# Spare matmuls on TensorE in the entry of a two-layer AdaLN kernel (17 of them, ahead of three waits)

## The reference, cut to what matters

```python
mod = (silu(c) @ wmod).reshape(8, 6, 1, 128)       # sa, ca, ga, sb, cb, gb
ga, gb = sign(.) * maximum(abs(.), 0.25)           # the two gates are clipped
h = layernorm(x) * (1 + ca) + sa
x = x + ga * attention(h)     # layer 0: 16 heads of 8, W + 2 * A.T B.T (LoRA) for q, k, v, o
h = layernorm(x) * (1 + cb) + sb
x = x + gb * moe(h)           # layer 0: 8 experts, top 2, and one shared; layer 1: SSM, conv + MoE
```

## Time and profile before

| | us |
|---|---|
| median of 3 runs | 1002.78 (998.81 to 1006.16) |
| the profiled execution | 1009.28 |
| its span, first to last instruction | 1007.5 |
| its mean granted TensorE clock | 0.909 |
| PE, DVE, ACT, POOL busy | 840.4, 738.3, 632.3, 496.3 |

### The profile page before, as it was taken

The page is one execution under the profiler, slowest core; times in us unless marked ns, Lnnn a source line. Parts: engine busy times, 40 slices in busy tenths (PEclk is TensorE's granted clock), DMA queues, the critical chain, the costliest instruction groups (busy, mean ns, idle before and its releaser), DMA issues.

```text
span 1007.5 us, 14225 instructions
## 1 busy us (share of the span) xinstructions
PE 840.4 (83%) x4630; PEld 461.7 (46%) x4630; DVE 738.3 (73%) x1561; ACT 632.3 (63%) x1113; POOL 496.3 (49%) x794
## 2 busy tenths in 40 slices
PE   5689999999988988887796999889946559977986
PEld 4312222222212222221475877777733247766774
DVE  6687878788888778862485888858749577966771
ACT  2157777877766777676484777566715736545562
POOL 3715282727265666355552167656657046653211
PEclk9669999999999999898798999999967878978997
DMA  7735454545536264102115266556360000000000
GB/s 238 153 107 186 91 182 97 166 112 152 125 120 160 107 172 124 68 24 109 52 36 177 97 221 247 195 190 217 115 237 10 24 1 1 0 1 11 22 21 32
DMA packets 45477, 110.78 MB, mean 110 GB/s; under 512 B 7886, under 2 KB 20814, under 8 KB 40086
## 3 DMA queue, kind: packets, MB, share of 16 engines
q1 hardware_dynamic: 39260, 97.93, 32.5%
q0 software_dynamic: 4992, 10.36, 3.0%
q10 hardware_dynamic: 1152, 1.58, 0.5%
HBM read 57.65 MB, written 51.03 MB: 108 GB/s over the span
## 4 chain that ended last, share of the span: by engine, by line
PE 49%; DVE 19%; issue 10%; POOL 10%; ACT 8%; DMA 4%; SPq 0%; another core or an unknown queue 0%; POOLq 0%; DVEq 0%; ACTq 0%
PE PS L1083 10%; DVE mx L891 9%; PE PS L1072 6%; PE PS L1053 4%; PE PS L320 4%; PE PS L322 3%; PE PS L321 3%; POOL yd L1298 3%; DMA HT<-xs 2%; ACT E L798 2%; PE PS L1035 2%; PE PS L1020 1%; ACT ov L804 1%; PE PS L2425 1%; PE PS L2428 1%
## 5 line engine op out<-in xcount | busy, mean ns | idle before, releaser
L891 DVE TENSOR_REDUCE mx<-PS 128x2 f32<-128x1024 f32 x256 | 305.5, 1221 | 76.4 <-PE PS L1053 70.6
L798 ACT ACTIVATE E<-PS 128x512 f32<-128x512 f32 x512 | 277.0, 599 | 85.8 <-PE PS L1072 81.7
L1072 PE MATMUL PS<-Q,K 51*128 51x512 bf16 x512 | 166.0, 396 | 10.6 <-ACT E L798 6.9
L1053 PE MATMUL PS<-K,Q 48*128 48x512 bf16 x512 | 140.6, 409 | 27.1 <-DVE mx L891 26.7
L1083 PE MATMUL PS<-E,V 128*9 128x512 f32 x1024 | 140.1, 620 | 19.5 <-ACT ov L804 18.8
L1298 POOL DMA_INDIRECT yd<-yt,goes x92 | 94.6, 1028 | 49.2 <-DVE yt L1474 25.6
L1072 PEld LDWEIGHTS PS<-Q,K 51*128 51x128 bf16 x512 | 37.0, 95 | 162.1 <-ACT E L798 97.2
L1462 DVE TENSOR_TENSOR Gl<-Gf,Gh 128x512 fp32r<-128x512 f32 x117 | 82.2, 719 | 31.6 <-ACT Gh L1333 22.1
L513 POOL DMA_INDIRECT xs<-HT,pos x64 | 63.8, 996 | 79.5 <-ACT E L798 45.2
L1327 ACT ACTIVATE Gf<-PS,WR 128x512 f32<-128x512 f32 x92 | 63.1, 689 | 48.7 <-PE PS L322 39.3
L2336 DVE SCALAR_TENSOR_TENSOR cb<-ye,gt,cb 128x128 f32<-128x128 f32 x224 | 65.5, 366 | 0.0
(11 more groups left out here) (420 smaller groups left out, 1895.1 us busy)
## 6 DMA issues: line engine op xcount, KB each, us to landing
WR<-wsd SPq DMA_DIRECT2D x23, 1028.0 KB
xs<-zero SPq DMA_DIRECT2D x8, 2112.0 KB, 7.4
wsd<-wsp SPq DMA_DIRECT2D x8, 1024.0 KB, 4.1
HT<-xs SPq DMA_DIRECT2D x23, 264.0 KB
dqk<-SPL SPq DMA_DIRECT2D x30, 192.0 KB, 2.8
Q<-dqk SPq DMA_DIRECT2D x14, 384.0 KB
K<-dqk SPq DMA_DIRECT2D x14, 384.0 KB
stage<-in_w SPq DMA_DIRECT2D x9, 516.0 KB
```

The costliest lines, as they stand in the source:

```text
L798: e.activation(E[:, m % 4, n % 4], PS[:, bank["exp", n], :], ACT.Exp).then_inc(*k.inc("exp", n))
L891: e.tensor_reduce(mx[:, 2 * s % 96:2 * s % 96 + 2], PS[:, o:o + 2, :], AX.X, ALU.max, negate=True).then_inc(*k.inc("max", s))
L1053: return e.matmul(PS[:, o + n % 2, :], Q[r, b % 3, h // 2, qt * P:(qt + 1) * P], K[r, b % 3, h // 2, :], start=True, stop=True)
L1072: e.matmul(PS[:, o, :], K[r, b % 3, h // 2, kt * P:(kt + 1) * P], Q[r, b % 3, h // 2, :], start=True, stop=True).then_inc(*k.inc("exp_mm", n))
```

## The change

Two things are new in PE's program. `warm(n)` issues n bf16 matmuls of a 128 x 128 stationary operand and 512 moving columns, both broadcast from the constant tile `half`, into the bank PVB. PE calls it three times: nine of them after a new wait for `const` and ahead of the wait for `small`; four between the LoRA products and the wait for `cs`; four between modulation(1) and zt(0). No semaphore is raised by them and nothing reads what they write. The tile `half` is float32 -0.5 read as pairs of bf16, of which the first is 0.0 and the second -0.5; the stationary operand takes the first of the pair, so every product is zero.

```diff
+                def warm(n):
+                    for _ in range(n):
+                        e.matmul(PS[:, PVB, :].rearrange("p (a n) -> p a n", a=8), half[:].bitcast(BF16)[:, 0:1].to_broadcast([P, P]),
+                                 half[:].bitcast(BF16).unsqueeze(1).to_broadcast([P, 8, 64]), start=True, stop=True)
+
+                k.wait_ge("const")
+                warm(9)
                 k.wait_ge("small")
                 for i in range(4):
                     m = e.matmul(PS[:, 1, i * P:(i + 1) * P], small[0:8, i * P:(i + 1) * P],
                                  small[0:8, (4 + i) * P:(5 + i) * P], start=True, stop=True)
                 m.then_inc(*k.inc("weff_mm"))
+                warm(4)
                 k.wait_ge("cs")
                 k.wait_ge("p0")
                 modulation(0)
                 modulation(1).then_inc(*k.inc("mod_mm", 0, 1))
+                warm(4)
                 zt(0)
```

## The result

Over 20 executions each the changed kernel takes 1007.01 us (999.66 to 1010.02) and the kernel before 1000.13 us (996.98 to 1006.16): a ratio of 1.0056, interval 1.0039 to 1.0073. I had forecast -0.8 us and a range up to 1006.5.

A forecast was written before the change was run, and what follows sets the result against it. PE, busy 83% with 49% of the chain, was taken to bound the entry up to modulation(5) at 11.57 us, at a low clock. An earlier rise gains 0.8 us net: 1002.78 - 0.8 = 1002.0, range 998.0 to 1006.5.

The forecast's parts named there:

- The entry: cost of warm(9), of the wait for const, and of both warm(4): PE's entry: warm(9) 3.9 us under the first load, cost 0; wait free; each warm(4) 1.72 us low clock, 0.86 full.
- Gains at a full clock: PE's entry: zt(0) 1.09 to about 0.55 us, modulation(2) to (5) 1.52 to 0.76; net gain taken as 0.8.
- When the clock would rise: PE's entry: 5.2 to 7.5 us after dense work starts, so at 6.2 to 8.5 us, middle 7.3.
- so it will be low again for batch 1, and the 11 us there cost what they cost now: PE's batch 1: clock falls again while PE idles, so its 11 us stay, give or take 0.9 us.
- After that nothing depends on the entry: Past the maxima's chain to expu at 59.39 us, the forecast claimed no further effect of the change.
- What is late next: After modulation(5): the DVE and POOL chain to 22.26 us moves by the 0.8 us, and the maxima start earlier.
- the slower one: Rival at modulation(5) on PE: spare matmuls cost more than they give, 0.5 to 2.2 us; time 1004.5; chance 0.2.
- The argument that no row shows zero products raising the clock: Support for the slower rival: products of a zero stationary operand may not raise PE's clock; only real work preceded rises.
- The spread gain: Rival in batch 1's projections: clock stays full into them, -4.8 us in all, 998.0; chance 0.05.
- Within 1%: Whole kernel: a measurement tells only about 10 us from no change; faster 0.03, same 0.94, slower 0.03.
- The sign of being wrong: Signs in the profile after: slow late zt(0), first reduction still at 33.5, clock never falling at 20 to 22 us.
- the last one named: Time prediction fails if executions after differ from those before by something not in the first 60 us.

The follow-up runs named there:

- tiny17_first: Kernel before plus 17 matmuls of 8 columns at the start of PE's program, ahead of the wait for small: 1006.61 us against 999.32, ratio 1.008.
- tiny17_mid: Kernel before plus 17 matmuls of 8 columns ending PE's attention stage, about 470 us in: 1004.59 us against 999.32, ratio 1.0046.
- after_pad111_mid: Changed kernel plus 111 matmuls of 8 columns at the end of the attention stage: 1004.13 us against 1001.16 for the kernel before, ratio 1.0027.
- the new order: SP asks for expert tokens one tile earlier, ahead of weights; against the kernel before: ratio 0.9943 (repeated, 0.9968) without the spare matmuls, 0.9946 with the change.
- after_pad111: Changed kernel plus 111 matmuls of 8 columns where PE waits for Z of batch 1: 1001.94 us against 1003.18 for the kernel before, ratio 0.9982.
- nine_only: Changed kernel without both warm(4), against the kernel before: 1001.42 us against 999.32, ratio 1.0013.

## Why the prediction was wrong

- **The entry: cost of warm(9), of the wait for const, and of both warm(4):** right. Nine take 4.02 us (3.9 forecast), four 1.02 to 1.04 at the high clock (0.86) and 1.72 to 1.82 at the low one.
- **Gains at a full clock:** right in the profiled execution (1.18 us, forecast 0.4 to 1.3), and not a gain of the median, since the clock rose early in three of five traces only.
- **When the clock would rise:** wrong as a range. Same code, same place: 4.8, 5.4, 5.5, 10.4 and 17.0 us. I took three rises of one execution for the spread of all. The first trace, at 5.4, is already outside 6.2 to 8.5.
- **"so it will be low again for batch 1, and the 11 us there cost what they cost now":** right; half of the 1.18 us was lost there.
- **"After that nothing depends on the entry":** this step failed, in "What is late next". It followed waits and left out what the added instructions themselves do: they move every later instruction fetch of PE. The sum for 17 matmuls had a term for their time and none for their number. Measured, that term is 5 to 7 us, some seven times the gain that was forecast: 17 small matmuls that change nothing in the entry cost 0.46% at 470 us, and asking for the tokens earlier brings both kernels to 994.
- **The rivals:** the slower one names a real case, at 13.55 against 13.8, but its place is the entry and it doesn't carry the loss: tiny17_first and tiny17_mid have no such delay and lose as much or more. Its time of 1004.5 is the nearest of the forecasts to the measured 1007.0, and that is luck. By its own terms a rise at 10.1 to 12.4 costs 0.4 to 1.5 us, not 0.5 to 1.8. The argument that no row shows zero products raising the clock is answered: they do. The spread gain did not occur; the clock was low again by 18.5 to 20.6 us in all the traces with 17 spare matmuls where it had risen early.
- **Within 1%:** right, as the measured 0.56% shows. But that a measurement can tell only 10 us from no change was wrong: over 20 executions each it told 5.6 us. The range missed by 0.5 us only because it stood on three executions of before with a median of 1002.78; over 20 that median is 1000.13, and against it the miss is 2.7 us larger.
- **The sign of being wrong:** the last one named, a difference that is not in the first 60 us, is what came. It had 0.03 of the chances.

What stays open: which places of the fetch are good and which are bad through the whole stage. Only 18, 34, 128, 192 and 256 instructions were tried, of which 34 and 128 cost. What fetches cost in the attention stage was not measured apart (after_pad111_mid). And the worth of the new order differs between two chips (0.57% and 0.32%).

## What to carry to other kernels

Before an instruction is called free, count it: in a long unrolled program like this one it shifts all later instruction fetches of its engine, and a stage whose loads land just in time can pay for that hundreds of microseconds on. A change of a few instructions that measures a few tenths of a percent needs a control with as many instructions that do nothing (and one with a whole block of them) before it is explained. The cure is slack at the load, not the right number: asking for the tokens a tile earlier made the three variants tried with it equal to each other within the noise of their chip, and the kernel 0.3 to 0.6% faster than before.

## What the runs showed of the hardware

- Small bf16 matmuls of 8 columns with a 128-column stationary operand take 0.03 to 0.04 us each in a row (17 in 0.61, 128 in 3.57, 111 in 2.92).
- One fetch of PE's program is one 16 KB packet for about 256 instructions, in a queue of its own (q8). It takes 0.9 to 2.1 us over the traces, mostly 1.0 to 1.2. Where it starts in the last 0.8 us of a load of weights, the tokens asked for behind it end 1.9 us after the weights and not 0.8.
- The granted clock printed ahead of the first recorded change is 1.00 although the durations are those of the 1.2 GHz level: in after_pad111 the LoRA products take 2.00 us under a printed 1.00, in the first trace of the change 1.24.
- Products of a zero stationary operand do raise the clock: in nine_only it rose at 4.1 us, when PE had done nothing else (its first other product starts at 5.11), and at 4.8 to 5.5 in three traces of the changed kernel. In two others of it the same work did not raise it before 10.4 and 17.0.
